# The first group's bias through DRAM instead of through two wide products, at the start of a four-layer kernel

## The chip, the cores and the metric

The kernel runs on one core of one Trainium2 chip. The metric is the time of one execution on the device, in microseconds (us). The times before are three runs; their median is compared with the median of the changed kernel.

## The reference

`x` has shape (64, 32, 512), which is 64 batches of 32 rows, and there is a condition vector of 128 numbers for each batch. Four layers follow each other, each of the form `x = x + ffn(cond(x))`. Only the first part of layer 0 matters here:

```
h = gelu(embedding @ W0 + b0)
h = gelu(h @ W1 + b1)
att = softmax(h @ W2 + b2)                       # (64, 8)
agg_w = einsum('bk,koi->boi', att, weight)       # one 32 x 32 matrix for each batch
agg_b = att @ bias_k                             # one bias of 32 numbers for each batch
out = einsum('boi,bih->boh', agg_w, x) + agg_b[:, :, None]
gate, up = out @ W_gate.T, out @ W_up.T          # 1792 columns each
x = x + (silu(gate) * up) @ W_down.T
```

Layers 2 and 3 have a `cond` of the same kind, layer 1 has a grouped convolution in its place.

## The kernel before

The 2048 rows of `x` are 16 tiles of 128 rows, and four tiles make a group (so a group is 16 batches, 512 rows). Each engine has its instruction stream written out by hand, in a function of its own; semaphores order them. There is no scheduler: the order in the code is the order on the engine.

The start goes like this. SyncE (SP) issues the loads `pack_a` (condition and first weights), `pack_d`, `pack_c` (mixing weights `wk`, bias table `kbias`, masks, identity) and `xs` (the first group's `x`). TensorE (PE) runs the small network on the condition; VectorE (DVE) and ScalarE (ACT) do gelu and softmax. Five products of `ones` with `ones` (lines 678 and 679), whose result nobody reads, stand between the network and what needs the softmax. The result, `att`, is spread by PE into `att_m` forms; DVE then builds for the first group the block-diagonal matrix `blk` (in two halves, semaphores `s_blk_half` and `s_blk[0]`), and PE multiplies `xs` by it: 16 products, the first 8 for tiles 0 and 1, the others for tiles 2 and 3, with one signal `s_cond_mm[0]` for each of four chunks of columns (lines 782 to 789). An fp32 product appears in the trace as two passes, so these are 32 passes.

The bias of the first group must stand in `bias_bc`, a [128, 512] tile with the same row in all 128 partitions. ACT copies the transposed attention to `attT` (line 1066); GpSimd (POOL) multiplies it with `kbias` into `terms` (line 556; `terms` lies in the buffer `silu` and is printed under that name); PE adds it over the partitions and spreads it at once, by a product of `ones` with `terms` of 512 columns (line 692); ACT copies the result to `bias_bc` (line 1071).

DVE then adds `bias_bc` to each of the four chunks and writes `cT` (line 1225), ACT rounds each to `c_hi` (line 1080), and POOL (chunks 0 and 2) and DVE (chunks 1 and 3) subtract to get `c_lo`. PE meanwhile makes the table of all biases, six small products with one signal (lines 791 to 798), which ACT copies to `btab` and SP writes to DRAM (line 419) for the later groups, whose bias comes back from there by DMA. Then PE begins the feed-forward: for each of 14 slices m of the weights, 16 passes `gate_up` with `c_hi` and `c_lo`, and 8 passes `down`. The slices `wl` (768 KB each) are loaded by POOL: three before `terms`, eleven after its `split_c(0)` (lines 551 to 560).

Of the kernel before, what the change touches and what calls it, by code (L numbers as in the profile page):

```python
# [15 lines left out]
F32 = mybir.dt.float32  # L16
F32R = mybir.dt.float32r
ALU = mybir.AluOpType
# [3 lines left out]
P = 128  # L22
D = 512
S = D // P
ROWS = 32
NB = 64
# [4 lines left out]
GB = GT * TB  # L31
# [4 lines left out]
M = FF // P  # L36
# [16 lines left out]
def build(nc, A, out):  # L53
    ctx = ExitStack()
    with ctx:
        def sb(name, shape, dt=F32):
            return ctx.enter_context(nc.sbuf_tensor(name, shape, dt))

        def sem(name):
            return ctx.enter_context(nc.semaphore(name))  # L60


        def views(t, *widths):

            at, out = 0, []
            for w in widths:
                out.append(t[:, at:at + w])
                at += w
            return out
# [9 lines left out]
        with ExitStack() as first:  # L79
            def sb0(name, dt):  # L80
                return first.enter_context(nc.sbuf_tensor(name, [P, 2, TOK], dt))

            silu, hff, h_hi, h_lo = sb0("silu", F32), sb0("hff", F32), sb0("h_hi", F32R), sb0("h_lo", F32R)
# [9 lines left out]
        bias_bc = sb("bias_bc", [P, TOK])  # L93
# [17 lines left out]
        wk, kbias, bmask, ident, cwT = views(pack_c, 3 * K * ROWS, 3 * ROWS, TB, P, ROWS)  # L111
# [3 lines left out]
        attT = sb("attT", [P, 3, NB])  # L115
        btab = sb("btab", [NB, 4, ROWS])
# [6 lines left out]
        ones = sb("ones", [P, P])  # L123
# [44 lines left out]
        y_dram = nc.dram_tensor("y_dram", (2, NB, ROWS * S, WIN), F32).ap()  # L168
        w_dram = nc.dram_tensor("w_dram", (ROWS, S, CB * P), F32).ap()
        x_dram = nc.dram_tensor("x_dram", (NB * ROWS, D), F32).ap()  # L170
        bias_dram = nc.dram_tensor("bias_dram", (NB, 4, ROWS), F32).ap()

        ps = ctx.enter_context(nc.psum_tensor("ps", [P, 8, 512], F32))

        def bank(i):
            return ps[:, i, :]
# [23 lines left out]
        def xT(g):  # L200

            if g < 2:
                return early_x[:, g * GT * D:(g + 1) * GT * D].rearrange("p (b n) -> p b n", b=TB)
            return xs[:] if g == 2 else osc[:]
# [7 lines left out]

            return xs if g % 2 else cT

        terms = silu[:, 0]
        prod0 = hff[:].rearrange("p b (j k o) -> p (b j) k o", k=K, o=ROWS)


# [21 lines left out]
        s_att_bc = sem("s_att_bc")  # L240
        s_att_turned = sem("s_att_turned")
        s_attT = sem("s_attT")
        s_terms = sem("s_terms")
        s_bias0 = sem("s_bias0")
        s_mix0 = sem("s_mix0")
        s_blk_half = sem("s_blk_half")
# [1 line left out]
        s_btab = sem("s_btab")  # L248
# [5 lines left out]
        s_bias_bc = [sem(f"s_bias_bc{i}") for i in range(2)]  # L254
# [102 lines left out]
        def _(sp):  # L357
# [49 lines left out]
            def fetch(g):  # L407
# [6 lines left out]
                for j in range(GT):  # L414
                    src = x_dram[(g * GT + j) * P:(g * GT + j + 1) * P].rearrange("(b i) n -> i b n", b=TB)
                    sp.dma_start(xT(g)[j * ROWS:(j + 1) * ROWS], src).then_inc(s_xT[g], 16)

            sp.wait_ge(s_btab, 2)
            sp.dma_start(bias_dram, btab[:]).then_inc(s_bias_dram, 16)
            sp.wait_ge(s_bias_dram, 16)  # L420
# [64 lines left out]
        def _(pool):  # L485
            pool.memset(wconv[:], 0.0).then_inc(s_wconv_zero, 1)

            def weights(m0, m1):

                for m in range(m0, m1):  # L490
                    pool.dma_start(wl0[:, m, :], A["wl0"][m]).then_inc(s_slice[m], 16)
# [18 lines left out]
            def split_c(g):  # L510

                for s in (0, 2):
                    pool.wait_ge(s_c_hi, S * g + s + 1)
                    pool.tensor_tensor(c_lo[:, s], cT[:, s], c_hi[:, s].bitcast(F32), ALU.subtract).then_inc(s_c_lo_even, 1)  # L514
# [18 lines left out]
            def mask(o, a, b, op):  # L533
# [15 lines left out]
                 slot.unsqueeze(1).broadcast_to([NB, G, TB]), ALU.mult)  # L549

            pool.wait_ge(s_pack_d, 16)
            weights(0, 3)

            pool.wait_ge(s_pack_c, 16)
            pool.wait_ge(s_attT, 1)
            pool.tensor_tensor(terms.rearrange("p (b o) -> p b o", o=ROWS),
                               attT[:, 0, 0:GB].unsqueeze(2).broadcast_to([P, GB, ROWS]),
                               kbias[:, 0:ROWS].unsqueeze(1).broadcast_to([P, GB, ROWS]), ALU.mult).then_inc(s_terms, 1)
            split_c(0)
            weights(3, M)  # L560
            pool.wait_ge(s_att_bc, 2)
            for q in range(1, G):
                mix(0, q)
# [88 lines left out]
            n = HALVES[0]  # L652
# [4 lines left out]
        def _(pe):  # L657
            def mm(o, l, r, start=True, stop=True):
                return pe.matmul(o, l, r, start=start, stop=stop)  # L659
# [15 lines left out]


            pe.wait_ge(s_set, 2)
            for n in range(5):
                mm(bank(7)[:, 0:P], ones[:], ones[:])
            pe.wait_ge(s_att, 7)  # L680
            mm(bank(3)[:, 0:NT * K], selrep, att_m[:, 0]).then_inc(s_att_spread, 1)
# [2 lines left out]
            pe.wait_ge(s_att, 9)  # L684
            mm(bank(2)[:, 0:NT * K], strip2[:].rearrange("b c o -> b (c o)"), att_m[:, 1])
            mm(bank(2)[:, NT * K:2 * NT * K], selrep, att_m[:, 2]).then_inc(s_att_spread, 1)
            for i in (1, 2):
                ins = pe.transpose(bank(1)[:, (i - 1) * NB:i * NB], att_m[:, i], ident[0:NB, 0:NB])
            ins.then_inc(s_att_turned, 1)

            pe.wait_ge(s_terms, 1)
            mm(bank(0), ones[:], terms).then_inc(s_bias0, 1)

            def nothing():
                pass
# [94 lines left out]

            pe.wait_ge(s_attT, 2)
            for l, i in COND.items():
                mm(bank(1)[0:NB, l * ROWS:(l + 1) * ROWS], attT[:, i], kbias[:, i * ROWS:(i + 1) * ROWS])
            mm(bank(1)[0:NB, ROWS:2 * ROWS], condT, cwT)
            for b in range(TB):
# [254 lines left out]
        def _(act):  # L1050
            def copy(o, i):
                return act.activation(o, i, ACT.Copy)  # L1052
# [11 lines left out]
            act.activation(att[:], att[:], ACT.Exp).then_inc(s_aexp, 1)  # L1064
            act.wait_ge(s_att_turned, 1)
            copy(attT[:, 0], bank(0)[:, 0:NB]).then_inc(s_attT, 1)
            act.wait_ge(s_att_turned, 2)
            copy(attT[:, 1:3].rearrange("p i n -> p (i n)"), bank(1)[:, 0:2 * NB]).then_inc(s_attT, 1)
            act.activation(scrap[:], scrap[:], ACT.Silu)
            act.wait_ge(s_bias0, 1)  # L1070
            copy(bias_bc[:], bank(0)).then_inc(s_bias_bc[0], 16)
            copy(att_bc[:, 1:3].rearrange("p i n -> p (i n)"), bank(2)[:, 0:2 * NT * K]).then_inc(s_att_bc, 1)
            act.wait_ge(s_mix0, 3)
            copy(att_bc[:, 0], bank(3)[:, 0:NT * K]).then_inc(s_att_bc, 1)
# [16 lines left out]

            split_c(0)
            act.wait_ge(s_bias_mm, 1)
            copy(btab[:].rearrange("b l o -> b (l o)"), bank(1)[0:NB, 0:4 * ROWS]).then_inc(s_btab, 1)
            copy(biasN, bank(1)[:, P:P + NT]).then_inc(s_biasN, 1)
            with act.Fori(0, G - 1) as g:
                layer0(g, True)
# [469 lines left out]
```

## Time and profile before

| | us |
|---|---|
| median of 3 runs | 542.66 |
| lowest and highest | 541.59, 543.32 |
| the profiled execution's own time | 542.93 |
| span of its trace, first to last instruction | 541.1 |

The profiled execution's own time is 1.8 us above its span and within the three runs. Times in the trace count from the first instruction. PE is busy for 529.0 us of the span. The names in the trace are those of the buffers without their numbers; line 659 is the helper that issues every matmul, line 1178 the one for DVE's tensor_tensor, and line 1052 ACT's copy.

### The profile page before, as it was taken

How to read it: one execution, taken by the hardware profiler on the slowest of the kernel's cores; microseconds unless marked ns; L12 is line 12 of the kernel's file. 1: busy time of each engine (PE TensorE's matmuls, PEld its weight loads, DVE VectorE, ACT ScalarE, POOL GpSimd, SP SyncE). 2: the span in 40 equal slices, each digit the busy share in tenths (PEclk: the TensorE clock that was granted, in tenths of full speed). 3: DMA queues.
4: the chain of work that ended last, by engine and by line, in shares of the span. 5: the costliest groups of instructions: out<-in, count | busy, mean ns of one | idle time of the engine just before them, and what ended most of it. 6: DMA issues, size and time to landing. Idle time of an engine off the chain costs nothing.

```text
span 541.1 us, 6961 instructions
## 1 busy us (share of the span) xinstructions
PE 529.0 (98%) x2643; PEld 393.3 (73%) x2643; DVE 240.8 (45%) x537; ACT 141.0 (26%) x247; POOL 157.4 (29%) x153
## 2 busy tenths in 40 slices
PE   7999999999999999999999999999999999989996
PEld 6888888888888888888888886635454444577784
DVE  3543322722223723223622224544525258897775
ACT  5422222322222322222322222000002217545232
POOL 3599992300000400000300930040002000127666
PEclk9999999999999999999999999999999999999999
DMA  8398440196000230000205000959696929599763
GB/s 307 122 419 314 141 102 0 40 164 125 0 0 0 72 102 0 0 0 0 86 14 136 1 1 0 153 130 166 190 192 173 221 40 222 110 165 212 179 137 118
DMA packets 82502, 61.60 MB, mean 114 GB/s; under 512 B 61744, under 2 KB 66864, under 8 KB 81712
## 3 DMA queue, kind: packets, MB, share of 16 engines
q1 hardware_dynamic: 77696, 41.83, 35.2%
q0 software_dynamic: 4704, 19.40, 14.1%
q8 instruction: 14, 0.23, 0.2%
q10 hardware_dynamic: 80, 0.08, 0.0%
q14 instruction: 8, 0.07, 0.0%
HBM read 38.98 MB, written 12.81 MB: 96 GB/s over the span
## 4 chain that ended last, share of the span: by engine, by line
PE 90%; DVE 6%; issue 1%; ACT 1%; DMA 1%; POOL 0%; DVEq 0%; POOLq 0%
PE ps L659 89%; DVE cT L1352 1%; DVE xs L1178 1%; DVE cT L1178 1%; DMA pack_a<-in_pack_a 1%; DVE c_lo L1178 0%; PE ps L858 0%; DVE c_lo_odd L1178 0%; PE ps L819 0%; DVE t L1178 0%; DVE rest L1369 0%; PE ps L973 0%; PE ps L872 0%; DVE wcat L1375 0%; DVE m L1365 0%
## 5 line engine op out<-in xcount | busy, mean ns | idle before, releaser
L659 PE MATMUL ps<-c_hi,wl 128*128 128x512 f32 x448 | 169.9, 389 | 0.0
L659 PE MATMUL ps<-c_lo,wl 128*128 128x512 f32 x448 | 169.7, 389 | 0.0
L1178 DVE TENSOR_TENSOR hff<-silu,ps 128x512 f32<-128x512 f32 x56 | 38.5, 688 | 164.3 <-PE ps L659 161.7
L659 PEld LDWEIGHTS ps<-c_lo,wl 128*128 128x128 f32 x448 | 84.1, 188 | 17.4
L659 PEld LDWEIGHTS ps<-c_hi,wl 128*128 128x128 f32 x448 | 84.0, 188 | 17.4
L659 PE MATMUL ps<-wl,h_hi 128*128 128x512 f32 x224 | 87.6, 391 | 0.0
L659 PE MATMUL ps<-wl,h_lo 128*128 128x512 f32 x224 | 87.2, 389 | 0.0
L1086 ACT ACTIVATE silu<-ps 128x512 f32<-128x512 f32 x56 | 33.5, 598 | 119.8 <-PE ps L659 119.6
L1052 ACT ACTIVATE h_hi<-hff 128x512 fp32r<-128x512 f32 x56 | 35.4, 632 | 107.4 <-DVE hff L1178 107.4
L1178 DVE TENSOR_TENSOR h_lo<-hff,h_hi 128x512 fp32r<-128x512 f32 x56 | 43.3, 773 | 39.1 <-ACT h_hi L1052 39.1
L659 PE MATMUL ps<-wbase,cT 128*128 128x512 f32 x128 | 56.5, 594 | 0.0
L514 POOL TENSOR_TENSOR c_lo<-cT,c_hi 128x512 fp32r<-128x512 f32 x8 | 10.7, 1342 | 156.3 <-ACT c_hi L1052 156.3
L659 PEld LDWEIGHTS ps<-wl,h_hi 128*128 128x128 f32 x224 | 42.1, 188 | 10.3 <-issue 1.7
L659 PEld LDWEIGHTS ps<-wl,h_lo 128*128 128x128 f32 x224 | 42.1, 188 | 8.6
L659 PEld LDWEIGHTS ps<-wbase,cT 128*128 128x128 f32 x128 | 23.7, 190 | 28.0 <-issue 28.0
L585 POOL TENSOR_TENSOR x_all<-x_all,bbase 128x512 f32<-128x512 f32 x16 | 21.9, 1405 | 31.1 <-DMA wlb<-in_wlb 31.0
L1233 DVE STREAM_TRANSPOSE tr<-ps 128x512 f32<-128x512 f32 x16 | 11.2, 708 | 34.3 <-PE ps L659 34.3
L576 POOL COPY prod<-x_all 128x512 f32<-128x512 f32 x16 | 10.1, 647 | 54.7 <-DVE x_all L1178 37.3
L507 POOL TENSOR_TENSOR prod<-prod 128x512 f32<-128x512 f32 (+1 forms) x22 | 25.2, 1147 | 1.7
L637 POOL TENSOR_TENSOR x_all<-x_all,t 128x512 f32<-128x512 f32 x15 | 20.6, 1381 | 11.7 <-DVE t L1178 9.3
L504 POOL TENSOR_TENSOR prod<-att_bc,pack_c 128x1024 f32<-128x1024 f32 x11 | 21.2, 1926 | 0.8
L1178 DVE TENSOR_TENSOR x_all<-x_all,ps 128x512 f32 (+1 forms) x32 | 19.9, 677 | 0.1
(179 smaller groups left out, 579.3 us busy)
## 6 DMA issues: line engine op xcount, KB each, us to landing
wl<-in_wl POOLq DMA_DIRECT2D x14, 768.0 KB, 9.2
stg<-y_dram SPq DMA_DIRECT2D x64, 128.0 KB, 5.0
xs<-in_x SPq DMA_DIRECT2D x4, 1024.0 KB, 8.5
x_all<-in_x SPq DMA_DIRECT2D x1, 4096.0 KB, 14.9
y_dram<-prod SPq DMA_DIRECT2D x16, 256.0 KB, 2.2
x_dram<-x_all SPq DMA_DIRECT2D x4, 1024.0 KB, 7.0
x_all<-cS POOLq DMA_DIRECT2D x4, 1024.0 KB, 7.7
x_all<-in_bias POOLq DMA_DIRECT2D x4, 1024.0 KB, 10.5
```

The costliest lines, as they stand in the source:

```text
L504: step(pool.tensor_tensor(prod[:], a.unsqueeze(3).broadcast_to([P, GT, K, ROWS]), wk[:, i].unsqueeze(1).broadcast_to([P, GT, K, ROWS]), AL ...
L507: step(pool.tensor_tensor(prod[:, :, 0:n], prod[:, :, 0:n], prod[:, :, n:2 * n], ALU.add))
L514: pool.tensor_tensor(c_lo[:, s], cT[:, s], c_hi[:, s].bitcast(F32), ALU.subtract).then_inc(s_c_lo_even, 1)
L576: pool.tensor_copy(halves_x[:, j % 2], x_all[:, j, :].rearrange("p (s c h) -> p h s c", s=S, h=2)).then_inc(s_parted, 1)
L585: pool.tensor_tensor(x_all[:, j, :], x_all[:, j, :], bbase[:], ALU.add).then_inc(s_base_bias, 1)
L637: pool.tensor_tensor(xg, xg, t1[:, j], ALU.add).then_inc(s_x_new[3], 1)
L659: return pe.matmul(o, l, r, start=start, stop=stop)
L1052: return act.activation(o, i, ACT.Copy)
L1086: act.activation(silu[:, m % 2], bank(4 + 2 * (m % 2)), ACT.Silu).then_inc(s_silu, 1)
L1178: return dve.tensor_tensor(o, a, b, op)
L1233: dve.transpose(tr[:, q % 2], bank(4 + q)).then_inc(s_turned1, 1)
L1352: dve.tensor_copy(cT2(g)[:, :, j * P:(j + 1) * P], bank(base2(g) + j).rearrange("p (s n) -> p s n", s=S)).then_inc(s_cT[2], 1)
```

## The change

The first group's bias no longer comes from `terms` and the wide product. PE computes `attT` times `kbias`, a product with 32 columns of output, into a free corner of bank 0; ACT copies it to `btab[:, 0]`; SP writes the first 16 rows of that to a new DRAM tensor `bias0_dram`, waits until it has landed, and reads it back, spread to all 128 partitions, into `bias_bc`. POOL's `terms` is gone. POOL issues two slices of weights at first, then waits for `bias_bc` to be filled, issues the next two, does its `split_c(0)`, and issues the other ten. One of the five idle products is gone. In the table of all biases, the product for layer 0 is left out, since `btab[:, 0]` is already there.

```diff
+            sp.wait_ge(s_btab0, 1)
+            sp.dma_start(bias0_dram, btab[0:GB, 0]).then_inc(s_bias0_dram, 16)
+            sp.wait_ge(s_bias0_dram, 16)
+            sp.dma_start(bias_bc[:], bias0_dram.rearrange("b o -> (b o)").unsqueeze(0).broadcast_to([P, GB * ROWS])).then_inc(s_bias_bc[0], 16)
             sp.wait_ge(s_btab, 2)
             sp.dma_start(bias_dram, btab[:]).then_inc(s_bias_dram, 16)
...
             pool.wait_ge(s_pack_d, 16)
-            weights(0, 3)
+            weights(0, 2)
 
             pool.wait_ge(s_pack_c, 16)
-            pool.wait_ge(s_attT, 1)
-            pool.tensor_tensor(terms.rearrange("p (b o) -> p b o", o=ROWS),
-                               attT[:, 0, 0:GB].unsqueeze(2).broadcast_to([P, GB, ROWS]),
-                               kbias[:, 0:ROWS].unsqueeze(1).broadcast_to([P, GB, ROWS]), ALU.mult).then_inc(s_terms, 1)
+            pool.wait_ge(s_bias_bc[0], 16)
+            weights(2, 4)
             split_c(0)
-            weights(3, M)
+            weights(4, M)
...
             pe.wait_ge(s_set, 2)
-            for n in range(5):
+            for n in range(4):
                 mm(bank(7)[:, 0:P], ones[:], ones[:])
...
             mm(bank(2)[:, NT * K:2 * NT * K], selrep, att_m[:, 2]).then_inc(s_att_spread, 1)
+            pe.wait_ge(s_attT, 1)
+            mm(bank(0)[0:NB, P:P + ROWS], attT[:, 0], kbias[:, 0:ROWS]).then_inc(s_bias0, 1)
             for i in (1, 2):
                 ins = pe.transpose(bank(1)[:, (i - 1) * NB:i * NB], att_m[:, i], ident[0:NB, 0:NB])
             ins.then_inc(s_att_turned, 1)
-
-            pe.wait_ge(s_terms, 1)
-            mm(bank(0), ones[:], terms).then_inc(s_bias0, 1)
...
             for l, i in COND.items():
+                if l == 0:
+                    continue
                 mm(bank(1)[0:NB, l * ROWS:(l + 1) * ROWS], attT[:, i], kbias[:, i * ROWS:(i + 1) * ROWS])
...
             copy(attT[:, 0], bank(0)[:, 0:NB]).then_inc(s_attT, 1)
+            act.wait_ge(s_bias0, 1)
+            copy(btab[:, 0], bank(0)[0:NB, P:P + ROWS]).then_inc(s_btab0, 1)
             act.wait_ge(s_att_turned, 2)
             copy(attT[:, 1:3].rearrange("p i n -> p (i n)"), bank(1)[:, 0:2 * NB]).then_inc(s_attT, 1)
             act.activation(scrap[:], scrap[:], ACT.Silu)
-            act.wait_ge(s_bias0, 1)
-            copy(bias_bc[:], bank(0)).then_inc(s_bias_bc[0], 16)
...
-            copy(btab[:].rearrange("b l o -> b (l o)"), bank(1)[0:NB, 0:4 * ROWS]).then_inc(s_btab, 1)
+            copy(btab[:, 1:4].rearrange("b l o -> b (l o)"), bank(1)[0:NB, ROWS:4 * ROWS]).then_inc(s_btab, 1)
```

On PE, between the idle products and the first group's products with `blk`, the order before was this (`strip` is the buffer of a selection mask, `silu` here is `terms`, and the brackets name the semaphores that a row waits for):

```order
L659 MATMUL ps<-ones 128x128 [waits s_set]
L659 MATMUL ps<-ones 128x128 x4
L659 MATMUL ps<-att_m,pack_b 128x128 [waits s_att]
L683 MATMUL ps<-pack_c,att_m 128x64 [waits s_pack_c]
L659 MATMUL ps<-att_m,strip 128x128 [waits s_att]
L659 MATMUL ps<-att_m,pack_b 128x128
L688 MATMUL ps<-pack_c,att_m 128x64 x2
L659 MATMUL ps<-silu,ones 128x512 [waits s_terms]
L659 MATMUL ps<-blk,xs 128x128 [waits s_blk_half,s_staged0]
```

In the changed kernel the same place reads:

```order
L662 MATMUL ps<-ones 128x128 [waits s_set]
L662 MATMUL ps<-ones 128x128 x3
L662 MATMUL ps<-att_m,pack_b 128x128 [waits s_att]
L686 MATMUL ps<-pack_c,att_m 128x64 [waits s_pack_c]
L662 MATMUL ps<-att_m,strip 128x128 [waits s_att]
L662 MATMUL ps<-att_m,pack_b 128x128
L662 MATMUL ps<-pack_c,attT 64x32 [waits s_attT]
L693 MATMUL ps<-pack_c,att_m 128x64 x2
L662 MATMUL ps<-blk,xs 128x128 [waits s_blk_half,s_staged0]
```

The wide product has gone from its place ahead of the `blk` products, and the small one stands ahead of two transposes.

On POOL, from the masks of the start to the first mixing step, the order before was:

```order
L536 TENSOR_TENSOR place<-group_sum,pack_b 64x16 [waits s_masks2]
L491 DMA wl<-in_wl 128x1536 [waits s_pack_d,s_masks2]
L491 DMA wl<-in_wl 128x1536 x2
L556 TENSOR_TENSOR silu<-attT,pack_c 128x512 [waits s_attT,s_pack_c]
L514 TENSOR_TENSOR c_lo<-cT,c_hi 128x512 [waits s_c_hi] x2
L491 DMA wl<-in_wl 128x1536 x11
```

And in the changed kernel:

```order
L541 TENSOR_TENSOR place<-group_sum,pack_b 64x16 [waits s_masks2]
L496 DMA wl<-in_wl 128x1536 [waits s_pack_d,s_masks2]
L496 DMA wl<-in_wl 128x1536
L496 DMA wl<-in_wl 128x1536 [waits s_bias_bc0,s_pack_c]
L496 DMA wl<-in_wl 128x1536
L519 TENSOR_TENSOR c_lo<-cT,c_hi 128x512 [waits s_c_hi] x2
L496 DMA wl<-in_wl 128x1536 x10
```

Two slices now stand behind a wait for the bias and ahead of `c_lo`.

SP's queue in the changed kernel, from the load of `xs` on (`bias_dram` in the second and third row is the new `bias0_dram`):

```order
L364 DMA xs<-in_x 128x4x512
L420 DMA bias_dram<-btab 16x32 [waits s_btab0]
L422 DMA bias_bc<-bias_dram 128x512 [waits s_bias0_dram]
L424 DMA bias_dram<-btab 64x128 [waits s_btab]
L427 DMA x_all<-in_x 128x16x512 [waits s_slice13,s_bias_dram]
```

The write and the read of the first group's bias are new; before, the table's write followed `xs` directly.

## Rows read from the trace of the kernel before

**Rows 1.** The page: busy time of PE, and the chain that ended last.
```profile
PE 529.0 (98%) x2643; PEld 393.3 (73%) x2643; DVE 240.8 (45%) x537; ACT 141.0 (26%) x247; POOL 157.4 (29%) x153
...
PE 90%; DVE 6%; issue 1%; ACT 1%; DMA 1%; POOL 0%; DVEq 0%; POOLq 0%
```

**Rows 2.** The chain that ended last, 0 to 60 us: start, us, what.
```profile
10.52 0.23 ACT attT L1052
...
10.89 1.05 POOL silu L556
...
11.99 48.23 PE ps L659 x226
```

**Rows 3.** Timeline of PE, 0 to 22 us: start, us, what, passes.
```profile
7.15 2.50 PE L659 MATMUL ps<-ones 128*128 128x128 f32 x10
9.59 0.79 PE L659 MATMUL ps<-att_m,pack_b 64*128 64x128 f32 x2
...
11.99 2.07 PE L659 MATMUL ps<-silu,ones 128*128 128x512 f32 x2 [0.33 <-POOL silu L556]
13.86 5.47 PE L659 MATMUL ps<-blk,xs 128*128 128x128 f32 x32
19.25 0.54 PE L659 MATMUL ps<-pack_c,attT 128*64 128x32 f32 x6
...
20.03 2.11 PE L659 MATMUL ps<-c_hi,wl 128*128 128x512 f32 x8
21.98 0.39 PE L659 MATMUL ps<-c_lo,wl 128*128 128x512 f32 x1
```

**Rows 4.** Timeline of PE, two windows: 13.9 to 17.2 us, 17.5 to 19.2.
```profile
13.86 3.62 PE L659 MATMUL ps<-blk,xs 128*128 128x128 f32 x16
...
17.27 2.05 PE L659 MATMUL ps<-blk,xs 128*128 128x128 f32 x16
```

**Rows 5.** Timeline of DVE, 0 to 30 us.
```profile
8.97 0.28 DVE L1178 TENSOR_TENSOR att_m<-pack_b,att 64x128 f32<-64x128 f32 x1
...
12.27 0.42 DVE L1178 TENSOR_TENSOR blk<-agg,pack_c 128x256 f32<-128x256 f32 x1
...
18.09 2.48 DVE L1178 TENSOR_TENSOR cT<-ps,bias_bc 128x512 f32<-128x512 f32 x4 [3.28 <-PE ps L659]
```

**Rows 6.** Timeline of ACT, 0 to 30 us.
```profile
18.81 2.42 ACT L1052 ACTIVATE c_hi<-cT 128x512 fp32r<-128x512 f32 x4 [3.61 <-DVE cT L1178]
21.14 0.26 ACT L1052 ACTIVATE btab<-ps 64x128 f32<-64x128 f32 x1
```

**Rows 7.** Timeline of POOL, 0 to 40 us.
```profile
6.05 1.83 POOL L491 DMA_DIRECT2D wl<-in_wl  x3 [0.36 <-POOL place L536]
...
19.52 2.99 POOL L514 TENSOR_TENSOR c_lo<-cT,c_hi 128x512 fp32r<-128x512 f32 x2 [7.58 <-ACT c_hi L1052]
22.46 5.87 POOL L491 DMA_DIRECT2D wl<-in_wl  x11
```

**Rows 8.** DMA issues: count, KB, us from issue to landing; first of the whole kernel.
```profile
pack_a<-in_pack_a SPq DMA_DIRECT2D x1, 227.0 KB, 2.8
...
bias_dram<-btab SPq DMA_DIRECT2D x1, 32.0 KB, 5.4
...
out_x<-x_all SPq DMA_DIRECT2D x2, 128.0 KB, 1.8
```

**Rows 9.** The same view of two windows: 372 to 373.7 us, 477 to 478.
```profile
bias_bc<-bias_dram SPq DMA_DIRECT2D x1, 256.0 KB, 5.7
...
bias_bc<-bias_dram SPq DMA_DIRECT2D x1, 256.0 KB, 3.7
```

**Rows 10.** Windows: stretch, us, busy by engine, PEclk, DMA share, GB/s.
```profile
14.00:15.00 1.00, 1.00 (x7) 1.00 (x6) 0.78 (x2) 0.84 (x3) 0.00 (x0) 1.00 0.41 147
15.00:16.00 1.00, 1.00 (x7) 1.00 (x7) 0.00 (x0) 0.20 (x2) 0.00 (x0) 1.00 0.09 31
...
24.00:28.00 4.00, 4.00 (x19) 3.32 (x18) 1.69 (x3) 1.59 (x3) 4.00 (x9) 1.00 1.15 415
```

More of the change, by code:

```diff
@@ L170, in build @@
         x_dram = nc.dram_tensor("x_dram", (NB * ROWS, D), F32).ap()
+        bias0_dram = nc.dram_tensor("bias0_dram", (GB, ROWS), F32).ap()
         bias_dram = nc.dram_tensor("bias_dram", (NB, 4, ROWS), F32).ap()
@@ L213, in cT3 @@
             return xs if g % 2 else cT
-        terms = silu[:, 0]
         prod0 = hff[:].rearrange("p b (j k o) -> p (b j) k o", k=K, o=ROWS)
@@ L242, in build @@
         s_attT = sem("s_attT")
-        s_terms = sem("s_terms")
+        s_btab0 = sem("s_btab0")
+        s_bias0_dram = sem("s_bias0_dram")
         s_bias0 = sem("s_bias0")
```

## The prediction, on record before the run

> **What bounds the kernel now.** I read the page first: PE is busy for 98% of the span and carries 90% of the chain that ended last [rows 1]. So whatever makes PE's long stream begin earlier should shorten the kernel by as much, and work on other engines is worth nothing unless PE waits for it. The change lies in the first 23 us, so next I read the chain there [rows 2]. It goes through exactly what is edited: ACT's copy of the attention (10.52), POOL's `terms` (10.89 to 11.94), then PE without a gap from 11.99. Last the timeline of PE [rows 3]: 0.33 us idle for `terms`, then the wide product in two passes, until 13.86, then the 32 passes with `blk`. DVE had the first half of `blk` done at 12.27 + 0.42 = 12.69 [rows 5]. Those passes stood in the queue behind the wide product for 13.86 - 12.69 = 1.17 us, and that is what the change can free. After them come the bias table (19.25) and the first feed-forward pass at 20.03.
>
> **PE's clock at that place.** The first 16 of the 32 passes take 17.27 - 13.86 = 3.41 us, or 0.213 us each; the last 16 take 19.25 - 17.27 = 1.98 us, or 0.124 us each [rows 3, 4]. These are the two levels, 1.2 and 2.4 GHz, although the granted clock reads 1.00 in all of this stretch [rows 10]; I go by the passes. PE had been in unbroken work since 11.99 when the clock rose. So work moved forward can slide from the fast stretch into the slow one, and a start that is earlier by 1 us may not give 1 us.
>
> **Part by part.**
>
> *One idle product less.* Five take 2.50 us, so one takes 0.50 with the drain of the last, or about 0.45 between starts. PE began the spreading product at 9.59 [rows 3]; its input was ready at 8.97 + 0.28 = 9.25 [rows 5]. With four, PE is free before 9.25, and the product can begin at about 9.30. Bounds: 0 (the weight load was hidden behind the idle products and comes into view) to 0.29. I take 0.25. DVE's chain to `blk` hangs on this product, so the first half comes at 12.45.
>
> *`terms` and the wide product away.* PE may begin the `blk` passes at 12.45 instead of 13.86, 1.41 us earlier. If the clock rises at the same moment, 17.27, then (17.27 - 12.45) / 0.213 = 22.6 passes run slowly and the other 9.4 at 0.124, so they end at 18.43: 0.82 us earlier than 19.25. If the rise moves along with the start, it is the full 1.41. I take 0.82, since nothing but the place in time is known of that rise.
>
> *The small product and its copy.* Three products of this shape take 0.54 us on PE [rows 3], so about 0.2 each. It stands ahead of two transposes and in front of the wait for `blk`, where PE now idles: nothing. One of the same shape leaves the bias table behind the passes, which spans 20.03 - 19.25 = 0.78 us for 16 passes, so 2 passes fewer give 0.1. The copy to `btab` costs ACT at most the 0.26 us of the larger one [rows 6], with ACT idle there.
>
> *The way through DRAM.* This replaces a path on the engines by two transfers in a row, and is the real question. The small product starts about 11.0 (attention copied at 10.52 + 0.23 [rows 2], less 0.25, then its place in PE's queue), the copy ends about 11.7, SP issues the write. For this write of 8 KB the trace has no row. Nearest: 1.8 us with idle queues, and 5.4 us for the 32 KB table, whose wait was spent while slices ran at a DMA share of 1.15 [rows 8, 10]. In the changed kernel only two slices are in flight. Before, three kept the engines busy into 15 to 16 us, where a share of 0.09 is left [rows 10]; a slice of 768 KB at 415 GB/s is 1.9 us, so now they fall idle before about 13.8. A write that has to let them all pass lands by then or shortly after; I take 2.3 us. For the read of 256 KB: 3.7 us for the same amount in 128-byte pieces, 5.7 under load [rows 9], 2.8 for 227 KB in long pieces [rows 8]. The new one reads 2 KB pieces, nearest to the last: 2.8. `bias_bc` is then full at 11.7 + 2.3 + 2.8, plus 0.1 of waits, about 16.9. Bounds: 11.7 + 1.8 + 2.8 = 16.3 and 11.7 + 5.4 + 5.7 = 22.8.
>
> The Trainium skill, "DMA: Bandwidth & Descriptors", section "Queues, rings and completion order", says each DMA engine takes turns between the queues that have work, a packet at a time. By that rule alone the write would not have to let the slices pass, and the bias would be there at 16.3. The 5.4 us of the table speak for a longer wait. Both lie ahead of the deadline below.
>
> *When the bias is needed.* DVE's first add waits for the 20th pass: 12.45 + 20 x 0.213 + 0.3 = 17.0. There is more room behind it. From bias to `c_hi` of the first chunk takes 18.81 - 18.09 + 0.63 = 1.35 us [rows 5, 6], and PE wants that only at 19.1 (18.43 + 0.78 - 0.1). So the bias costs nothing until 17.75, and everything gained is used up at 20.03 - 1.35 = 18.7; later than that, each microsecond costs one.
>
> *POOL and the slices.* POOL's `split_c` now stands behind the bias and two issues (1.83 / 3 = 0.61 each [rows 7]): free at 16.9 + 1.3 = 18.2. `c_hi` of chunk 0 comes at 17.0 + 1.35 = 18.35. So `c_lo` isn't held; at a bias later than about 17.6 it would be. Its two take 2.99 us and end about 21.4. PE wants chunk 2 of `c_lo` after eight passes and four more, about 1.95 + 1.0 us from its start at 19.1, so at 22.0. Room 0.6. Slices 2 and 3 are issued near 17 to 18, before 22.46 as now, except that slice 2 was issued by 7.9 until now; PE reaches it only after two slices' `gate_up` and one `down`, 40 passes of some 0.23 us = 9 us after 19.1. The remaining slices come earlier than before, POOL's mixing too, since POOL's `split_c` moves forward with the chain. The two new rows in SP's queue delay nothing: the next, the table at 23, is long after.
>
> **Sum.** 0.82 for the passes and 0.1 for the table: 0.92 us off a span of 541.1, so 540.2. The profiled execution's own time is 542.93, near the median 542.66; from the median I come to 541.75, rounded to 541.8.
>
> **Rivals.** What a measurement of this kernel can tell from no change is about 0.3%, 1.6 us.
>
> *The clock rises earlier too.* PE's dense work begins 1.41 us sooner, and if the rise follows it, the gain is 1.41 + 0.1 = 1.5 us: 541.15. Against it: between the last small product and `blk` PE will idle for about 0.8 us, where it idled for 0.33. Chance 0.15; a fifth of it, with noise, would read as faster.
>
> *The clock rises later.* The wide product gave PE 2.07 us of dense work before the passes; without it dense work begins at 12.45, not 11.99. All 32 passes slow are 6.8 us and end at 19.27, as now, and some of the feed-forward would run at half speed: eight slow passes of 0.23 us cost 1.8 us. Gain between 0.7 (rise later by 0.46) and a loss of 1.7; middle -0.5: 543.2. The Trainium skill, "TensorE: Matmul & The Clock Gate", section "What's actually happening", holds that the clock is throttled by default and released by activity, by which an idle product or a wide one earns something. The rows lend that little: five idle products from 7.15 had not raised the clock by 13.86, for the 16 passes after it are slow [rows 3, 4]. Chance 0.18.
>
> *The bias comes late (the slower side).* The mechanism is the write waiting behind the slices as the table's did, and a read like those under load: bias at 22.8, feed-forward at 24.15, 4.1 us later than now: 546.8, and up to 1.8 more if the clock falls meanwhile, 548.6. It decides from 18.7 on. For it: 5.4 and 5.7 are real rows. Against it: both were measured with traffic that is not there after 13.8. Chance 0.08.
>
> *No gain at all.* Something else paces the start, such as the chain DVE, ACT, POOL up to `c_lo` with its 0.6 us of room, and it remains 542.7. Chance 0.09. The forecast itself has 0.50.
>
> **Range.** 80% between 541.0 (full shift and a little noise) and 543.3 (late clock). The three runs before spread over 1.7 us. Faster by over 0.3% takes 541.03 or less, which no mechanism here reaches by itself: 0.08. Slower by over 0.3%: 0.08, from the late bias and a part of the late clock. Same: 0.84.
>
> **What would show it.** In the trace after: PE's spreading product at about 9.3; the `blk` passes from about 12.45, with 22 or 23 of them slow; `bias_bc` landed by 17, and DVE's first add released by PE, not by the transfer; first feed-forward pass at 19.1; `c_lo` of POOL not released by the DMA issues. I am wrong if the add begins later than 17.8, if the passes are all slow, or if the feed-forward starts where it did.

## The result, and the profile after

Over 20 runs each, the changed kernel takes 543.38 us (542.67 to 545.17) and the kernel before 542.20 (540.82 to 543.32). The ratio is 1.0019, 95% interval 1.0012 to 1.0025: by that ratio about 1.0 us slower (the medians lie 1.18 apart). That is inside the 0.3% that I called no change, but outside my range, and the wrong way round. The profiled execution took 543.07 us, its span is 541.3.

The chain that ended last, 0 to 60 us (start, us, what), answers to [rows 2]:

```profile
11.67 2.66 DMA bias_dram<-btab
...
14.34 3.18 DMA bias_bc<-bias_dram
...
17.55 2.48 DVE cT L1182 x4
20.03 2.22 DVE c_lo L1182
...
22.29 37.83 PE ps L662 x165
```

PE is no longer what carries the start. The chain runs through both transfers, then DVE's adds and its first `c_lo`, and reaches PE only at 22.29. Timeline of PE, 0 to 22 us, against [rows 3]; the last row is the window 23.5 to 23.9:

```profile
9.21 0.79 PE L662 MATMUL ps<-att_m,pack_b 64*128 64x128 f32 x2
...
12.45 5.29 PE L662 MATMUL ps<-blk,xs 128*128 128x128 f32 x32 [0.64 <-DVE blk L1182]
17.67 0.42 PE L662 MATMUL ps<-pack_c,attT 128*64 128x32 f32 x4
...
18.95 2.53 PE L662 MATMUL ps<-c_hi,wl 128*128 128x512 f32 x8 [0.56 <-ACT c_hi L1056]
...
23.79 0.39 PE L662 MATMUL ps<-c_hi,wl 128*128 128x512 f32 x1
```

PE's part went as wanted: `blk` starts at 12.45, and the passes end 1.58 us sooner than before (17.67 against 19.25). Part of that is luck: read from the spacing of the passes (0.21 us slow, 0.11 fast), the clock rose at 15.57 in this trace and at 17.48 in the one of before. Then PE waits 0.56 us for `c_hi`. The last row is the seventeenth feed-forward pass, the first of slice 1. In the trace of before it also stood at 23.79:

```profile
23.79 0.39 PE L659 MATMUL ps<-c_hi,wl 128*128 128x512 f32 x1
```

All that was gained at 17.67 is gone there. Timelines of DVE and POOL, 17 to 30 us; the second DVE row is its window at 19.9:

```profile
17.55 2.48 DVE L1182 TENSOR_TENSOR cT<-ps,bias_bc 128x512 f32<-128x512 f32 x4 [3.12 <-DMA bias_bc<-bias_dram]
19.95 2.29 DVE L1182 TENSOR_TENSOR c_lo<-cT,c_hi 128x512 fp32r<-128x512 f32 x1
...
18.05 1.07 POOL L496 DMA_DIRECT2D wl<-in_wl  x2 [10.81 <-DMA bias_bc<-bias_dram]
19.11 2.57 POOL L519 TENSOR_TENSOR c_lo<-cT,c_hi 128x512 fp32r<-128x512 f32 x2
```

DVE's adds wait for the transfer, not for PE. And DVE's first `c_lo` takes 2.29 us. It ends at 22.24, after both of POOL's, and PE wants it second in line. The same instruction in the trace of before:

```profile
20.49 0.87 DVE L1178 TENSOR_TENSOR c_lo<-cT,c_hi 128x512 fp32r<-128x512 f32 x1
```

### The profile page after: what moved, and what is told of

It is laid out like the page before. It is cut to its first block, busy times and chain, and to the rows that moved or that the text cites. A ratio compares the mean times of both kernels' runs of the same rounds, so it can differ in the third digit from the quotient of the medians.

```text
span 541.3 us, 6953 instructions
## 1 busy us (share of the span) xinstructions
PE 527.9 (98%) x2639; PEld 391.7 (72%) x2639; DVE 246.2 (45%) x537; ACT 140.5 (26%) x247; POOL 156.0 (29%) x152
## 4 chain that ended last, share of the span: by engine, by line
PE 88%; DVE 7%; DMA 2%; issue 1%; ACT 1%; DVEq 0%
PE ps L662 87%; DVE cT L1182 1%; DVE cT L1356 1%; DVE xs L1182 1%; DVE c_lo L1182 1%; DMA bias_bc<-bias_dram 1%; DMA pack_a<-in_pack_a 1%; DMA bias_dram<-btab 0%; PE ps L862 0%; DVE c_lo_odd L1182 0%; PE ps L823 0%; DVE t L1182 0%; DVE rest L1373 0%; PE ps L977 0%; PE ps L876 0%
## 5 line engine op out<-in xcount | busy, mean ns | idle before, releaser
L1182 DVE TENSOR_TENSOR h_lo<-hff,h_hi 128x512 fp32r<-128x512 f32 x56 | 48.3, 863 | 39.1 <-ACT h_hi L1056 39.1
L1182 DVE TENSOR_TENSOR x_all<-x_all,ps 128x512 f32 (+1 forms) x32 | 19.9, 677 | 0.1
```

Of the source, the lines that this page charges most:

```text
L1182: return dve.tensor_tensor(o, a, b, op)
```

## The experiments

**Two more traces, one of each kernel, unchanged.** What was expected of the kernel before, and of the changed one:

> The kernel before, unchanged, for a second trace of it. Theory A (its start is paced by TensorE, so it depends on when TensorE's clock rises, and the first trace showed a late rise at the 17th of the 32 blk passes): with an earlier rise the first feed-forward pass comes earlier than 20.03, by up to 1.4 us, and the second slice's first pass earlier than 23.79; with the same rise the same. Theory B (nothing but noise outside the start): the start is as in the first trace whatever the clock does.

> The changed kernel, unchanged, for a second trace. Theory A (its start is paced by the bias on its way through DRAM and by the c_lo chain on VectorE and GpSimd): the bias lands again at about 17.5, the second slice's first gate pass is again within 0.3 us of 23.8, whenever the clock rises. Theory B (VectorE's 2.29 us for its first c_lo is an accident of that run): it takes under 1 us here and that pass comes about 0.6 us earlier.

The kernel before took 541.89 us, span 540.1 (PE, 0 to 22 us, and the window 22.5 to 22.8):

```profile
13.72 4.42 PE L659 MATMUL ps<-blk,xs 128*128 128x128 f32 x32
18.85 2.11 PE L659 MATMUL ps<-c_hi,wl 128*128 128x512 f32 x8
...
22.61 0.39 PE L659 MATMUL ps<-c_hi,wl 128*128 128x512 f32 x1
```

The same 32 passes take 4.42 us in place of 5.47: the clock rose about 2 us earlier (15.19 against 17.48). All behind them comes 1.18 us earlier, the seventeenth feed-forward pass too. The changed kernel took 543.60, span 541.5 (PE, then DVE):

```profile
12.50 6.11 PE L662 MATMUL ps<-blk,xs 128*128 128x128 f32 x32 [0.64 <-DVE blk L1182]
...
17.76 2.48 DVE L1182 TENSOR_TENSOR cT<-ps,bias_bc 128x512 f32<-128x512 f32 x4 [3.28 <-DMA bias_bc<-bias_dram]
20.16 2.89 DVE L1182 TENSOR_TENSOR c_lo<-cT,c_hi 128x512 fp32r<-128x512 f32 x2
```

Here the clock rose later (17.32), the passes took 6.11 instead of 5.29, and yet bias, `c_lo` and the seventeenth pass (24.00) come as before, 0.2 us later throughout. PE was ready for the feed-forward only at 19.20 and did not wait for `c_hi` this time, only for `c_lo`. From the first to the seventeenth feed-forward pass it takes 3.76 us in both traces of before, 4.84 and 4.80 in those of the changed kernel. Theory A holds for both: the kernel before is paced by PE's clock, the changed one by the bias and `c_lo`. The first trace of before had shown it at its slow end (542.93 against a median of 542.20).

**The bias at once, from an input.** It leaves out the first group's own bias.

```diff
             sp.dma_start(xs[:], xd[:, 0:GT, :]).then_inc(s_staged[0], 16)
+            sp.dma_start(bias_bc[:], A["bbase"]).then_inc(s_bias_bc[0], 16)
...
-            sp.wait_ge(s_bias0_dram, 16)
-            sp.dma_start(bias_bc[:], bias0_dram.rearrange("b o -> (b o)").unsqueeze(0).broadcast_to([P, GB * ROWS])).then_inc(s_bias_bc[0], 16)
...
-            pool.wait_ge(s_bias_bc[0], 16)
+            pool.wait_ge(s_bias0_dram, 16)
```

> The changed kernel with the first group's bias filled from a kernel input right behind the load of xs, with no dependence on the small product (the first group gets another layer's bias, the computation of its own bias is left out); GpSimd's wait for the bias becomes a wait for the landing of the small write, so its slices and its c_lo are issued as before or earlier. Theory A (the bias through DRAM is the last to arrive, TensorE waits 0.56 us for it through c_hi): VectorE's first add is released by TensorE near 16.5 to 17, the first feed-forward pass comes at about 18.4, some 0.5 us earlier, and the time falls by 0.5 to 1.1 us against the changed kernel, to about that of before, 542.2 to 542.9. Theory B (only the collision in c_lo matters): the adds come earlier, but the time stays within 0.3 us of the changed kernel's.

543.04 us, ratio to before 1.0016 (1.0006 to 1.0025). The start went as theory A said: DVE's adds at 16.65, the first feed-forward pass at 18.47, and `c_lo` without its long row. But the time hardly fell, where theory A wanted 542.2 to 542.9. The trace shows a second loss further on (DVE and POOL, window 23 to 28):

```profile
24.27 2.50 DVE L1181 TENSOR_TENSOR h_lo<-hff,h_hi 128x512 fp32r<-128x512 f32 x1 [0.70 <-ACT h_hi L1055]
...
22.62 3.74 POOL L495 DMA_DIRECT2D wl<-in_wl  x7
26.29 2.24 POOL L508 TENSOR_TENSOR prod<-att_bc,pack_c 128x1024 f32<-128x1024 f32 x1
```

The first `h_lo` takes 2.50, until 0.48 us after POOL's first mixing step has begun, and PE waits 0.7 us for it. In the trace of before it was:

```profile
25.78 0.69 DVE L1178 TENSOR_TENSOR h_lo<-hff,h_hi 128x512 fp32r<-128x512 f32 x1 [0.70 <-ACT h_hi L1052]
```

POOL is early in this kernel, so it reaches that step before DVE is past `h_lo`.

**Only one idle product less.**

```diff
-            for n in range(5):
+            for n in range(4):
```

> The kernel before with one idle product less and nothing else. Theory A: the spreading product comes at about 9.25 instead of 9.59, but terms and the wide product hang on the same chain, so all moves by 0.3 us and the ratio to before is 0.9995. Theory B (the idle products earn a clock that rises earlier): the rise comes later on the mean and the time is up to 0.7 us longer, ratio 1.000 to 1.0013.

542.25 us, ratio 0.9998 (0.9989 to 1.0006). The `blk` passes start at 13.54 instead of 13.86 or 13.72. The interval holds theory A's 0.9995 and the lower half of theory B's 1.000 to 1.0013; at most it says that the product costs less than 0.6 us either way.

**POOL's `c_lo` ahead of slices 2 and 3.**

```diff
-            pool.wait_ge(s_bias_bc[0], 16)
-            weights(2, 4)
             split_c(0)
-            weights(4, M)
+            weights(2, M)
```

> The changed kernel with GpSimd's split_c of the first group ahead of slices 2 and 3 instead of behind them, and without its wait for the bias. Theory A (the two issues delayed GpSimd's first c_lo by about 0.15 us, so that VectorE's first c_lo lost its turn between GpSimd's two and took 2.29 us; TensorE waited for it): VectorE's first c_lo takes about 0.9 us, the second slice's first gate pass comes near 23.0 instead of 23.8, and the time falls by 0.6 to 0.8 us, to about 542.7. Theory B (the late bias alone sets that pass): within 0.2 us of the changed kernel.

542.95 us, ratio 1.0007 (0.9998 to 1.0016), against 1.0019 for the changed kernel. DVE (window at 20.1) and PE (window at 23.4), in a run in which the clock rose late:

```profile
20.16 0.94 DVE L1180 TENSOR_TENSOR c_lo<-cT,c_hi 128x512 fp32r<-128x512 f32 x1
...
23.42 0.40 PE L660 MATMUL ps<-c_hi,wl 128*128 128x512 f32 x1
```

Bias at 17.76 as in the second trace of the changed kernel; but `c_lo` takes 0.94, and the seventeenth pass comes 0.58 us before that trace's 24.00. So about 0.6 us of the loss is the turn that DVE lost (the trace shows it; the two ratios' intervals still overlap). It may be a little more: from the first to the seventeenth pass it takes 3.96 us here against 4.80. POOL's first `c_lo` began at 19.27 here and at 19.32 there, with DVE's at 20.16 in both: a lead of 0.05 us, or the issues just ahead, decides who is next. Which of the two is not shown, only that moving the issues away gives DVE its turn back. The edit also moves the first mixing step from 27.08 to 28.51, so the first `h_lo` takes 0.69 again; what that was worth is looked at below.

**Four slices ahead in the kernel before.**

```diff
-            weights(0, 3)
+            weights(0, 4)
...
-            weights(3, M)
+            weights(4, M)
```

> The kernel before with four slices ahead of terms and ten behind c_lo, instead of three and eleven; nothing else. Theory A (a VectorE instruction that reads only SBUF is held up by the last of GpSimd's slice issues, and the first h_lo falls among those as soon as the issues end within about 2 us of it): the issues end 0.5 us earlier, h_lo takes 1.5 to 2.5 us instead of 0.69, and the time is 0 to 0.7 us above before, TensorE having about 0.95 us of room. Theory B (in the kernel with the early bias it was something else about that kernel): h_lo takes 0.69 us and the ratio is 1.000.

543.61 us, ratio 1.0016 (1.0007 to 1.0024). Nothing of the bias was touched, and the loss is the one of the kernel with the early bias (DVE and POOL, window 25 to 30):

```profile
25.91 2.38 DVE L1178 TENSOR_TENSOR h_lo<-hff,h_hi 128x512 fp32r<-128x512 f32 x1 [0.70 <-ACT h_hi L1052]
...
24.70 3.19 POOL L491 DMA_DIRECT2D wl<-in_wl  x6
27.85 2.22 POOL L504 TENSOR_TENSOR prod<-att_bc,pack_c 128x1024 f32<-128x1024 f32 x1
```

So one issue less behind `c_lo` is enough to cost 0.9 us. I took it for the work of the last issues themselves.

**The same, with the first mixing step held until `h_lo` is done.** The issues are left where they were.

```diff
+            pool.wait_ge(s_h_lo, 1)
             pool.wait_ge(s_att_bc, 2)
             for q in range(1, G):
```

> The kernel before with four slices ahead and ten behind (543.6 when measured, its first h_lo took 2.38 us), and besides GpSimd's first mixing step waits for the first h_lo. Theory A (the issues of the slices hold h_lo up): h_lo still takes about 2 us, until the last issue ends, and the time stays, ratio 1.001 to 1.002. Theory B (the mixing step that stands behind the issues, not the issues, holds it up): h_lo takes 0.69 us and the ratio falls to 1.000.

542.62 us, ratio 0.9998 (0.9987 to 1.0009). The interval just touches that of the run before it; the trace is clearer. The window 25 to 30 again:

```profile
25.45 0.69 DVE L1179 TENSOR_TENSOR h_lo<-hff,h_hi 128x512 fp32r<-128x512 f32 x1 [0.70 <-ACT h_hi L1053]
...
24.79 2.67 POOL L491 DMA_DIRECT2D wl<-in_wl  x5
27.42 2.00 POOL L504 TENSOR_TENSOR prod<-att_bc,pack_c 128x1024 f32<-128x1024 f32 x1
```

My theory A fell. `h_lo` runs right through the issues in 0.69 us; it is the mixing step that stands behind them, ready to go, that held it up. How it does that is open. In the five traces in which the first `h_lo` was long (1.06 to 2.50 us) it ended 0.44 to 0.48 us after that step began, and had begun about 2.0 us or less before it. In the trace of before, with 2.5 us between the two starts, it was not held.

**Three slices ahead of the bias.**

```diff
-            weights(0, 2)
+            weights(0, 3)
...
-            weights(2, 4)
+            weights(3, 4)
```

> The changed kernel with three slices ahead of the wait for the bias, as before the change, and one behind it. Theory A (the small write waits until the slices ahead have passed): it lands about 1.9 us later, near 16.2 instead of 14.3, the bias near 19.4, and the time rises by 1.5 to 2 us, to about 545. Theory B (queues take turns and the write does not wait for all of them): it lands within 0.5 us of 14.3 and the time stays.

545.79 us, ratio 1.0062 (1.0047 to 1.0076). The chain that ended last, and in a second view one of its windows (stretch, us, busy by engine, PEclk, DMA share, GB/s):

```profile
11.89 4.41 DMA bias_dram<-btab
...
16.32 3.22 DMA bias_bc<-bias_dram
```

```profile
22.40:25.80 3.40, 3.40 (x9) 2.55 (x9) 2.23 (x3) 0.52 (x3) 3.40 (x5) 0.50 0.52 175
```

The write took 4.41 us and the bias came at 19.5, 2.0 us later than in the changed kernel. Theory A held: the write landed at 16.30, and the last slice ahead of it had landed at 16.13. In the changed kernel the two times are 14.32 and 14.13. This is that kernel's second slice among the DMA issues (window 6.8 to 6.9; it was issued at 6.66):

```profile
wl<-in_wl POOLq DMA_DIRECT2D x1, 768.0 KB, 7.5
```

The load of `xs`, ahead of the write in SP's own queue, was over by 10.6 in both, so it is not what the write waited for. PE idled 2.4 us for `c_hi`, until 20.97, and the granted clock stood at 0.50 from 22.4 to 25.8, so the feed-forward passes in there ran at 1.2 GHz. By the ratios the time rose by 2.3 us: a late bias costs more than its own delay.

**Early bias, and the last ten slices issued after the first `h_lo`.** The first group's own bias is left out here too.

```diff
+            pool.wait_ge(s_h_lo, 1)
             weights(4, M)
```

> The kernel with the early bias of another layer (the first group's own bias left out), and besides GpSimd issues its last ten slices only when VectorE has finished the first h_lo. Theory A (in the kernel with the early bias h_lo took 2.50 us because of the last issues, and TensorE waited 0.7 us for it): h_lo takes 0.69 us, no wait there, and the time falls by 0.7 to 1 us against that kernel, to 542.0 to 542.3, a ratio to before of 0.9995 or less. Theory B: the time stays at 543.0.

542.64 us, ratio 0.9997 (0.9988 to 1.0006), against 1.0016 with the early bias alone. `h_lo` takes 0.69 us and PE waits for nothing behind 12.5. Expected was 0.9995 or less; the interval holds it, but a gain is not shown.

**All three losses answered.**

```diff
-            weights(0, 2)
+            weights(0, 1)
...
-            weights(2, 4)
+            weights(1, 2)
             split_c(0)
+            weights(2, 4)
+            pool.wait_ge(s_h_lo, 1)
             weights(4, M)
```

> The changed kernel with the three losses answered: one slice ahead of the wait for the bias instead of two, slices 2 and 3 behind GpSimd's c_lo instead of ahead of it (slice 1 alone stands between), and the last ten issued only after VectorE's first h_lo. Theory A (a late bias, a c_lo that loses its turn and an h_lo held up by the last issues are all that ate the gain): the small write lands near 13.4 and the bias near 16.6, VectorE's first add is released by TensorE, no wait of TensorE for c_lo or h_lo, and the time is that of the kernel with early bias and late issues, 542.0 to 542.6, a ratio to before of 0.999 to 1.000. Theory B (the way through DRAM has another cost): it stays at 1.001 or more.

542.30 us, ratio 0.9993 (0.9981 to 1.0005). The two transfers among the DMA issues (KB, us to landing), and DVE's adds in the timeline:

```profile
bias_bc<-bias_dram SPq DMA_DIRECT2D x1, 256.0 KB, 3.1
bias_dram<-btab SPq DMA_DIRECT2D x1, 2.0 KB, 1.3
```

```profile
17.23 2.60 DVE L1184 TENSOR_TENSOR cT<-ps,bias_bc 128x512 f32<-128x512 f32 x4 [2.73 <-PE ps L664]
```

The write lands in 1.3 us with one slice ahead, against 2.7 with two and 4.4 with three. The one slice ahead of it had landed at 12.31; the write, issued at 11.74, landed at 13.08. DVE waits for PE again. The whole way through DRAM is hidden, and its ratio is 0.0026 below the changed kernel's, but not shown to be better than before.

**Six idle products at the very start, in the kernel before and in the last one.**

```diff
+            pe.wait_ge(s_set, 2)
+            for n in range(6):
+                mm(bank(7)[:, 0:P], ones[:], ones[:])
             pe.wait_ge(s_pack_a, 16)
```

> The kernel before with six more idle products of ones at the very start, where TensorE waits for the first load until 3.6 us. Theory A (the start is paced by TensorE at its lower clock until about 15 to 17.5, and more work before that raises it sooner): the clock rises before the wide product, that product takes 0.9 us instead of 1.9 and the 32 blk passes 4 us instead of 5.4, the first feed-forward pass comes near 17 to 18 and the time falls by 1 to 2 us, ratio 0.996 to 0.998. Theory B (what counts is unbroken dense work just before the rise, and the small products from 3.6 to 7 do not give that): the rise stays where it was and so does the time.

> The kernel of one_slice_spread with the same six idle products at the very start. Theory A: if the clock rises sooner, the blk passes end near 16.5, but VectorE's adds wait for the bias near 16.6, so the first feed-forward pass comes at about 18 and the time is 0 to 0.6 us below one_slice_spread. Theory B (the rise is not moved): the same as one_slice_spread.

The kernel before with them: 542.57 us, ratio 0.9991 (0.9977 to 1.0004), with single runs from 540.08 to 543.25. In its trace (PE, 0 to 14 us, then the window 12 to 13) five idle products take 1.38 us instead of 2.50, so the clock had risen by then:

```profile
1.09 2.93 PE L659 MATMUL ps<-ones 128*128 128x128 f32 x12 [1.09 <-DVE ones L1183]
...
6.53 1.38 PE L659 MATMUL ps<-ones 128*128 128x128 f32 x10
...
10.83 1.31 PE L659 MATMUL ps<-silu,ones 128*128 128x512 f32 x2 [0.81 <-POOL silu L556]
```

```profile
12.00:13.00 1.00, 1.00 (x6) 1.00 (x5) 0.96 (x2) 0.76 (x3) 0.00 (x0) 0.50 1.16 424
```

It did not last. PE idled 0.87 us before the spreading product and 0.81 before the wide one, the granted clock then read 0.50, and the first 15 of the 32 `blk` passes ran slowly again. They began at 11.94, though, and the first feed-forward pass came at 17.86, 2.2 us sooner than in the first trace of before.

The last kernel with them: 541.80 us, ratio 0.9979 (0.9968 to 0.9990). It is the only version here that is faster than both kernels beyond its interval. In its trace the idle products still ran slowly (four in 2.08 us), so the early rise came in one of the two traces; theory A holds in part. What makes this kernel faster than the one without the six products is not shown: its ratio's interval overlaps that of the last kernel without them (0.9981 to 1.0005).

## Why the prediction was wrong, step by step

**The part of PE held.** The spreading product came at 9.21 (about 9.3 predicted), `blk` at 12.45 (12.45). That the passes ended 1.58 us earlier (0.82 if the clock rose at the same place, 1.41 if it moved along) was luck with the clock: in the second trace of the changed kernel they ended at 18.54, which is 0.71 earlier than in the first trace of before and 0.47 later than in the second.

**The first step that failed: the start of before was taken from one execution.** I read the clock's rise at the seventeenth `blk` pass and priced everything against it. The second trace had it some 2 us earlier and the first feed-forward pass at 18.85. Among five traces of kernels that still have the wide product (without the six early idle products), that pass stands at 18.53 to 20.12 (mean 19.44). The forecast of 19.1 for the changed kernel was thus no gain of 0.9 us over a typical execution of before, only of 0.3. The row of three runs beside the trace, 541.59 to 543.32 with the profiled one at 542.93, could have told me.

**The second: "the bias costs nothing until 17.75".** The write was sized 2.3 us and took 2.66; the read was sized 2.8 and took 3.18; the bias came at 17.5, not 16.9. (The write is 2 KB, not the 8 KB of the prediction.) That alone is within the stated room, but the room was not there: in the execution in which the clock rose early, PE was ready at 18.4 (18.14 + 0.26), and waited until 18.95. In the second trace it was ready at 19.20 and lost nothing here. The part of the mechanism was right: the write does wait for the slices ahead. In all six traces with two or three slices ahead it landed 0.2 us after the last of them. The Trainium skill's rule of turns between queues ("DMA: Bandwidth & Descriptors", "Queues, rings and completion order"), by which the prediction put the bias at 16.3, would not give this by itself. The last slice was expected at 13.8 and landed at 14.13.

**The third, and the largest: "`c_lo` isn't held ... Room 0.6".** It counted when POOL would be done (21.4; it was 21.68) and took DVE's `c_lo` as unchanged. DVE's first took 2.29 us instead of 0.87 and cost about 0.6 us, shown by moving POOL's `c_lo` ahead of the issues. Together with what the late bias does there, the stretch from the first to the seventeenth feed-forward pass lost 1.04 to 1.08 us, where the prediction has nothing. This was in none of my rivals by name; "something else paces the start", with 0.09, is the nearest.

**The fourth: "POOL's mixing comes earlier" at no cost.** It costs when its first step catches DVE's first `h_lo`. With the early bias PE waited 0.7 us for that. In the changed kernel `h_lo` took 1.56 us, but this cost next to nothing: from the seventeenth pass to the end of the span there are 517.5 us in both its traces, 517.3 and 517.5 in the two of before, and 518.6 with the early bias.

**Together.** The changed kernel is 1.0 us slower; with all three losses answered 1.4 us come back (0.9993), and the two intervals, 1.0012 to 1.0025 and 0.9981 to 1.0005, lie apart. How it splits is less sure: by the ratios 0.65 us go to `c_lo` put first (1.0007) and 0.75 to the rest, but in the traces the seventeenth pass moves by 0.58 us with the first and by 0.27 with the second, and the intervals of these steps overlap. What then remains of the 0.92 us gain is about 0.4 us, not told from nothing. That fits the traces: first feed-forward pass at 19.0 on the mean in the three in which PE waits for nothing ahead of it (18.47, 19.14, 19.39), 19.44 in the five with the wide product.

Why it is not 0.9 stays open. My second rival has the clock rise later without the wide product. The rise stands at 14.76 to 17.67 us (mean 16.3) in the five traces with it and at 15.57 to 17.93 (mean 16.7) in seven without it, the runs with early idle products left out of both. These ranges overlap nearly whole, so the rival is neither shown nor ruled out.

## What to carry to other kernels

Take more than one trace before pricing a saving of a microsecond at a kernel's start, where the clock's rise wanders by 2 to 3 us between executions: the place of the rise is part of the baseline. When work is taken off one engine, list what the others will then do at the same time as the critical instruction; here both hidden losses were a DVE instruction with all its operands in SBUF beside a GpSimd instruction whose start had moved a little (0.84 us between POOL's first `c_lo` and DVE's against 0.97 before; 2.0 us between `h_lo` and the mixing step against 2.5). A small transfer on a chain wants its neighbours' transfers issued behind it, not ahead.

## What the runs showed of the hardware

- A DVE subtraction of 128x512 with all operands in SBUF takes 0.69 us alone and up to 2.5 us beside a GpSimd tensor operation, or with one next in GpSimd's queue, while a product with one operand in PSUM (`hff`) takes 0.67 to 0.69 us each time. In five traces the held instruction ended 0.44 to 0.48 us after the GpSimd operation had begun. It ran in 0.69 us while GpSimd issued slices, when the tensor operation behind these had still to wait for a semaphore (542.62 us against 543.61 without that wait). What the queued operation holds is open.
- A write of 2 KB from SP landed in 1.3, 2.7 and 4.4 us behind one, two and three slices of 768 KB issued by GpSimd some 5 us earlier. What counts is when the last slice lands: in the six traces with two or three slices the write landed 0.2 us after it, also in the two with the early bias, whose load of 256 KB made slices and write later (4.0 and 3.7 us). Reading those 2 KB back to 128 partitions took 3.1 to 3.3 us in every run.
- With three slices ahead TensorE idled 2.44 us until 20.97, and its granted clock then stood at 0.50 between 22.4 and 25.8.
